# Low-rank network: two inner blocks side by side in TensorE's rows, ranks made twice, row steps two slots apart, and the later statistics taken there

## The reference

```
x = x + ratio_attention(layernorm(x))        # layer 0, causal, score = dot*dot / (|q|^2 + |k|^2 - 2 dot)
x = x + lowrank_ffn(layernorm(x))            # layer 0
x = x + zeroed_attention(layernorm(x))       # layer 1, masked scores are zeroed, not dropped
x = x + ternary_ffn(layernorm(x))            # layer 1, weights rounded to -1, 0, 1
```

```
P = layernorm(x) @ U1          # 256 -> 64
H = gelu(P @ V1 + b1)          # 64 -> 1024
out = (H @ U2) @ V2 + b2       # 1024 -> 64 -> 256
```

## Time and profile before

| | us |
|---|---|
| median of 3 executions | 3095.98 (3095.21 to 3100.54) |
| the profiled execution | 3089.9 |
| its span, first to last instruction | 3088.2 |
| first DMA issue of the low-rank stage | 1312.3 |
| first instruction of the zeroed attention | 1635.3 |
| first dot products of the zeroed attention | 1663.8 |

### The profile page before, as it was taken

How to read it: one execution, slowest core, us unless ns; L and a number is a source line. 1 busy time by engine, 2 the same in 40 slices (tenths; PEclk the granted TensorE clock), 3 DMA queues, 4 the chain that set the end, 5 groups by cost and what they waited for, 6 DMA issues and landing times. The chain is left out here.

```text
span 3088.2 us, 76579 instructions
## 1 busy us (share of the span) xinstructions
PE 2804.2 (91%) x28474; PEld 1973.6 (64%) x28516; DVE 2346.0 (76%) x6131; ACT 2041.1 (66%) x3686; POOL 1749.8 (57%) x3054
## 2 busy tenths in 40 slices
PE   5999999999999999879996888888888889699998
PEld 3777777777777777623333666666666667466666
DVE  6999999999999998753225666676666766399998
ACT  5999999999999999722331555555555555377776
POOL 4767776666666666532111555555555555466664
PEclk8999999999999999989997999999999999799999
DMA  4433443333343333110003544454535453000001
GB/s 108 72 72 73 72 72 72 71 70 69 67 71 69 69 61 65 29 46 1 0 0 72 85 83 75 76 82 79 79 73 86 70 87 65 2 8 28 21 22 35
DMA packets 110034, 181.96 MB, mean 59 GB/s; under 512 B 26720, under 2 KB 96096, under 8 KB 97568
## 3 DMA queue, kind: packets, MB, share of 16 engines
q1 hardware_dynamic: 106208, 176.28, 31.3%
q10 hardware_dynamic: 3456, 0.79, 0.2%
HBM read 115.92 MB, written 60.29 MB: 57 GB/s over the span
## 5 line engine op out<-in xcount | busy, mean ns | idle before, releaser
L792 POOL TENSOR_TENSOR ratio_scores<-ratio_scores,ratio_max_cols 128x512 f32<-128x512 f32 (+3 forms) x1024 | 729.0, 729 | 318.9 <-DVE ratio_max_cols L702 316.7
L1297 DVE TENSOR_REDUCE zeroed_max_cols<-bank 128x1 f32<-128x512 f32 (+3 forms) x1024 | 446.3, 481 | 192.1 <-PE bank L185 190.5
L1189 ACT ACTIVATE zeroed_prob<-bank 128x512 f32<-128x512 f32 x640 | 376.9, 593 | 305.1 <-PE bank L1078 210.1
L182 PE MATMUL bank<-ratio_k_stack,ratio_q_stack 102*128 102x512 bf16 (+7 forms) x2048 | 508.5, 303 | 29.2 <-DVE ratio_max_cols L702 13.3
L702 DVE CUSTOM_DVE_ANT_0 ratio_scores<-bank,ratio_scores 128x512 f32<-128x512 f32 (+3 forms) x1024 | 472.4, 489 | 22.2
L564 ACT ACTIVATE ratio_prob<-bank 128x512 f32<-128x512 f32 x640 | 379.5, 593 | 105.7 <-PE bank L478 105.5
L692 DVE TENSOR_TENSOR ratio_scores<-bank,ratio_inverse 128x512 f32<-128x512 f32 x640 | 435.7, 681 | 17.0 <-PE bank L182 9.8
L1410 POOL TENSOR_SCALAR_AFFINE_SELECT zeroed_prob<-zeroed_prob 128x256 f32<-128x256 f32 (+1 forms) x640 | 228.2, 365 | 338.5 <-ACT zeroed_prob L1189 336.9
L475 PE MATMUL bank<-const_f_sb,ratio_scores 128*128 128x128 f32 x2560 | 410.0, 274 | 0.7 <-ACT ratio_prob L564 0.7
L185 PE MATMUL bank<-const_b_sb 128*128 128x128 bf16 x2048 | 391.7, 223 | 0.0
L553 ACT ACTIVATE ratio_inverse<-bank 128x512 f32<-128x512 f32 x640 | 382.4, 598 | 12.6 <-PE bank L185 12.5
(11 more groups left out here) (169 smaller groups left out, 5574.4 us busy)
## 6 DMA issues: line engine op xcount, KB each, us to landing
ratio_q_stack<-ratio_parts_q SPq DMA_DIRECT2D x186, 128.0 KB
ratio_k_stack<-ratio_parts_k SPq DMA_DIRECT2D x186, 128.0 KB
zeroed_q_stack<-zeroed_parts_q SPq DMA_DIRECT2D x186, 128.0 KB, 4.4
zeroed_k_stack<-zeroed_parts_k SPq DMA_DIRECT2D x186, 128.0 KB, 7.5
ratio_parts_q<-ratio_parts SPq DMA_DIRECT2D x96, 128.0 KB
ratio_parts_k<-ratio_parts SPq DMA_DIRECT2D x96, 128.0 KB
zeroed_parts_q<-zeroed_parts SPq DMA_DIRECT2D x96, 128.0 KB
zeroed_parts_k<-zeroed_parts SPq DMA_DIRECT2D x96, 128.0 KB
```

Of the source, the lines that this page charges most:

```text
L182: i = e.matmul(bank[:, off:off + w], qs[0:rows, s, hh, ib * P:(ib + 1) * P], ks[0:rows, s, hh, 0:w], start=(k == 0), stop=mask is None, sk ...
L792: i = e.tensor_tensor(seg, seg, mx[:, pair % M_BUFS, c:c + 1].to_broadcast([P, w]), ALU.subtract)
L1189: e.activation(prob[:, n % FOLD_PROBS, 0:wd], exp_banks[n % 2][:, 0:wd], ACT.Exp, scale=0.25).then_inc(s["prob"])
L1297: i = e.tensor_reduce(mx[:, pair % FOLDS, c:c + 1], bank[:, off:off + (ib + 1) * P], AX_X, ALU.max)
```

## The change

- `up` now runs in every second slot and issues two matmuls: block f from partitions 0 to 63 of V1 and P, block f+1 from partitions 64 to 127, into two different banks. V1 is loaded twice, into both halves of the partitions. U1 is loaded twice side by side, so that `rank` makes P twice, in partitions 0 to 63 and 64 to 127 (a weight of 128 instead of 64 columns), and `keep_rank` copies 128 partitions. There are four banks for the inner blocks instead of two, and two instead of four for `down`.
- A row's preparation moves from slots 1, 2, 3 to slots 2, 4, 6, `out` from 3, 4 to 3, 5, and there are four buffers for normalised tiles instead of two, so both `normal` of a row run in slots 0 and 1. `keep_sums` stands ahead of the preparation.
- Weight steps are now in the odd slots from the second row on.
- The mean and variance that the zeroed attention needs are taken by DVE at the end of each row in the low-rank stage (slots 4 and 7), and no longer in the zeroed attention. There ACT's root moves from slot 5 to slot 1 and `normal` from slots 6, 9 to 5, 8.

```diff
-Z_STATS_AT, Z_ROOT_AT, Z_XN_AT, Z_TURN_AT, Z_VALUES_AT, Z_SPLIT_AT, Z_SUFFIX_AT, Z_GATHER_AT = (1, 2), 5, (6, 9), (8, 11), (0, 3), (13, 16), 19, 19
+Z_ROOT_AT, Z_XN_AT, Z_TURN_AT, Z_VALUES_AT, Z_SPLIT_AT, Z_SUFFIX_AT = 1, (5, 8), (8, 11), (0, 3), (13, 16), 19
...
                 if half % 2 == 0 and half + 2 < halves:
-                    if at in Z_STATS_AT:
-                        net.pair_stats(q, half // 2 + 1, Z_STATS_AT.index(at), net.stats_in, s["bn_stats"], s["bn_aggr"])
...
-            for pair in range(2):
-                net.pair_stats(q, 0, pair, net.stats_in, s["bn_stats"], s["bn_aggr"])
...
-    PREP_AT = {"xa": 1, "xb": 2, "rank": 3}
+
+    PREP_AT, OUT_AT, STATS_AT = {"xa": 2, "xb": 4, "rank": 6}, (3, 5), (4, 7)
...
-        if b < B - 1:
-            return 4 * b + f - 4 if f >= 4 else -1
-        return 4 * (B - 1) + f if f < FC else -1
+        return 4 * (b - 1) + f // 2 if b and f % 2 else -1
...
-        h_banks, prep_bank, post_bank, down_banks = bk[0:2], bk[2], bk[3], bk[4:8]
-        loaded = 16 * 7
+        h_banks, prep_bank, post_bank, down_banks = bk[0:4], bk[4], bk[5], bk[6:8]
+        loaded = 16 * 9
...
-                    i = e.matmul(prep_bank[0:RANK, :], u1[:, c, :], xnT[:, b % 2, c, :], start=(c == 0), stop=(c == 1))
+                    i = e.matmul(prep_bank[:, :], u1[:, c, :], xnT[:, b % 2, c, :], start=(c == 0), stop=(c == 1))
...
-                q.wait_ge(s["gelu"], n - 1)
-                e.matmul(h_banks[n % 2][:, :], v1[:, f * P:(f + 1) * P], rank_in[:, b % 2, :],
-                         start=True, stop=True).then_inc(s["up"])
+                q.wait_ge(s["gelu"], n - 2)
+                for k in range(2):
+                    rows = slice(k * RANK, (k + 1) * RANK)
+                    i = e.matmul(h_banks[(n + k) % 4][:, :], v1[rows, (f + k) * P:(f + k + 1) * P], rank_in[rows, b % 2, :],
+                                 start=True, stop=True)
+                i.then_inc(s["up"])
...
-                q.wait_ge(s["prep_filled"], prep[b, "xa"] if pair else prep[b - 1, "xb"] if b else 0)
+                q.wait_ge(s["prep_filled"], prep[b - 1, ("xa", "xb")[pair]] if b else 0)
...
             for n in range(n_slots + FC):
                 b, f = divmod(n, FC)
+                if b and f == 2:
+                    keep_sums(b - 1)
                 if b + 1 < B:
                     prepare(b + 1, f)
+                if b and f in OUT_AT:
+                    add(b - 1, OUT_AT.index(f))
+                if b and f in STATS_AT:
+                    pair = STATS_AT.index(f)
+                    q.wait_ge(s["post_read"], post(b - 1, pair))
+                    net.pair_stats(q, b - 1, pair, net.stats_out, s["out_stats"], s["out_aggr"])
                 if n < n_slots:
                     quantise(weight_step(n))
-                if b and f == 2:
-                    keep_sums(b - 1)
-                if b and f in (4, 5):
-                    add(b - 1, f - 4)
...
-            e.dma_start(u1[:, :, :], args["U1"].rearrange("(c p) r -> p c r", p=P)).then_inc(s["weights"], 16)
-            e.dma_start(v1[:, :], args["V1"]).then_inc(s["weights"], 16)
+            for k in range(2):
+                e.dma_start(u1[:, :, k * RANK:(k + 1) * RANK], args["U1"].rearrange("(c p) r -> p c r", p=P)).then_inc(s["weights"], 16)
+            for k in range(2):
+                e.dma_start(v1[k * RANK:(k + 1) * RANK, :], args["V1"]).then_inc(s["weights"], 16)
```

More of the change, by code:

```diff
@@ L1582, in turn_x @@
                 q.wait_ge(s["prep_read"], prep[b, ("xa", "xb")[pair]] - 1)
-                turn_blocks(e, prep_bank, lambda t: xn[:, t % 2, :], pair, net.ident).then_inc(s["prep_filled"])
+                turn_blocks(e, prep_bank, lambda t: xn[:, t, :], pair, net.ident).then_inc(s["prep_filled"])
             def rank(b):
@@ L1637, in out @@
                 i.then_inc(s["post_filled"])
-            for f in range(4):
-                prepare(0, f)
+            turn_x(0, 0)
+            turn_x(0, 1)
+            rank(0)
             for n in range(n_slots + FC):
                 b, f = divmod(n, FC)
-                if n < n_slots:
+                if n < n_slots and n % 2 == 0:
                     up(n)
@@ L1651, in pe @@
                     quantise(weight_step(n))
-                if b and f in (3, 4):
-                    out(b - 1, f - 3)
+                if b and f in OUT_AT:
+                    out(b - 1, OUT_AT.index(f))
         def act(q):
@@ L1660, in act @@
                 q.wait_ge(s["weights"], loaded)
[L1661 removed]
+                q.wait_ge(s["up"], n // 2 + 1)
                 q.wait_ge(s["down"], (n - H_BUFS) // 2 + 1)
[L1663 removed]
+                e.activation(hidden[:, n % H_BUFS, :], h_banks[n % 4][:, :], ACT.Gelu_apprx_tanh,
                              bias=b1[:, f:f + 1]).then_inc(s["gelu"])
@@ L1692, in keep_rank @@
                 q.wait_ge(s["prep_filled"], prep[b, "rank"])
-                q.wait_ge(s["up"], (b - 1) * FC)
-                e.tensor_copy(rank_in[:, b % 2, :], prep_bank[0:RANK, :]).then_inc(s["prep_read"])
+                q.wait_ge(s["up"], (b - 1) * (FC // 2))
+                e.tensor_copy(rank_in[:, b % 2, :], prep_bank[:, :]).then_inc(s["prep_read"])
             def prepare(b, f):
-                if f in (1, 2):
-                    keep_x(b, f - 1)
                 if f < 2:
                     normal(b, f)
-                if f == 3:
+                if f == PREP_AT["xa"]:
+                    keep_x(b, 0)
+                if f == PREP_AT["xb"]:
+                    keep_x(b, 1)
+                if f == PREP_AT["rank"]:
                     keep_rank(b)
@@ L1734, in dve @@
             e.reciprocal(scale[:, :], scale[:, :]).then_inc(s["scale"])
-            for f in range(4):
-                prepare(0, f)
+            normal(0, 0)
+            normal(0, 1)
+            keep_x(0, 0)
+            keep_x(0, 1)
+            keep_rank(0)
             for n in range(n_slots + FC):
                 b, f = divmod(n, FC)
+                if b and f == 2:
+                    keep_sums(b - 1)
                 if b + 1 < B:
                     prepare(b + 1, f)
+                if b and f in OUT_AT:
+                    add(b - 1, OUT_AT.index(f))
[3 more added lines that the diff above has]
+                    net.pair_stats(q, b - 1, pair, net.stats_out, s["out_stats"], s["out_aggr"])
                 if n < n_slots:
                     quantise(weight_step(n))
-                if b and f == 2:
-                    keep_sums(b - 1)
-                if b and f in (4, 5):
-                    add(b - 1, f - 4)
         def pool(q):
```

30 lines of the change are left out of this document (15 added, 15 removed).

## The result

| | before | changed kernel |
|---|---|---|
| median of 4 executions, us | 3095.6 (3092.45 to 3100.54) | 2969.23 (2964.26 to 2970.16) |
| profiled execution, us | 3089.9 | 2970.16 |
| its span, us | 3088.2 | 2968.4 |
| start to the low-rank stage, us | 1312.3 | 1317.3 |
| low-rank stage | 322.9 | 262.3 |

The ratio is 0.9594, 95% interval [0.9574, 0.9614]: 4% faster. The forecast was 2984.5, range 2958 to 3020. A stage counts from its first DMA or table load to that of the next. The first stage has the same code before and after; it took 1312 to 1318 us in the profiles of this case, so its 5.0 us are no effect of the change, and stages shouldn't be read finer than that. The span fell by 60.6 + 63.2 + 1.0 - 5.0 = 119.8 us.

A forecast was written before the change was run, and what follows sets the result against it. PE's queue was taken to bound low-rank rows, DVE the heads of zeroed-attention rows. Gains 62 + 7.5 - 2 + 44 = 111.5 from 3089.9 gave 2978.4; with the median 6.1 above, 2984.5 us, range 2958 to 3020.

The forecast's parts named there:

- Up pairs: Low-rank stage: a pair of ups side by side costs 1.10 us; row 13.65 against 17.52, 62 us gained in 16.
- The covers named: Low-rank row: waits cost nothing; `keep_rank` lies under a down, gelus under down and up, DVE's row 7.3 of 13.65 us.
- Rivals 1 and 2: Low-rank up pairs: 1, staggered by half a matmul, 1.48 us, 3009, chance 0.12; 2, no overlap, 1.91, 3036, chance 0.08.
- Weights and POOL: Early low-rank rows: of 23.5 us, 12 of POOL stalls and 4 from DVE's weight steps remain; net gain 7.5.
- Start and statistics: Low-rank stage: first rank 1.2 us later, first gelu 1, loss 2; last row's statistics move 1.0 us, nothing gained.
- Zeroed attention: Attention rows: 1.98 us of DVE statistics removed, 29.7 in 15 rows, plus 14 from the clock; 44 (25 to 58).
- rival 3: Zeroed attention: another wait refills PE's idle time and the clock still falls; 44 becomes 10, 3018 us, chance 0.10.
- Rival 4: Low-rank stage: PE drops to 1.2 GHz for whole rows, 13.65 us more each; all 16 give 3203, chance 0.03.

The follow-up runs named there:

- series kernel: The changed kernel, but both ups of a pair use partitions 0 to 63 of V1 and P; 3017.23 us.
- four kernels: Statistics in the attention with `normal` late 3025.27 us, early 2991.13; statistics in the low-rank stage with `normal` late 2976.9, early (changed kernel) 2969.23.
- kernel with waits of 1.5 us: The changed kernel with only the attention's slots of root and `normal` put back to 5 and 6, 9; 2976.9 us.

## Why the prediction was right, and where its sizes were off

*Up pairs: right.* 1.06 against 1.10 taken, between ends of 1.05 and 1.91. The row is 13.48 against 13.65: 4.04 less than before, times 16 = 64.6 us (62 forecast). The covers named held: DVE has 7.23 of 13.48 us, and PE waits for `keep_rank` 1.0 us in the whole stage. Rivals 1 and 2 are refuted by the 1.06, and the series kernel, which has the same order of steps and 1.92 a pair, shows that the different rows of the array do it. The first rival read a pair of 1.48 out of the rule in the Trainium skill, "TensorE: Matmul & The Clock Gate", Part 3, that matmuls start and end in program order; the 1.06 does not bear out that reading.

*Weights and POOL: the step that failed.* The forecast came out near the measured time, but this term did not: I forecast that 12 + 4 us of stalls would be left of 23.5; the ranks say 24.8.

Timeline of the changed kernel, ranks of rows 2 and 5, in answer to the earlier trace rows:

```profile
1354.57 1.98 PE L1582 MATMUL bank<-lowrank_xn_T,lowrank_u_twice 128*128 128x512 f32 x4
...
1419.77 1.99 PE L1582 MATMUL bank<-lowrank_xn_T,lowrank_u_twice 128*128 128x512 f32 x4
```

1419.77 - 1354.57 = 65.20, less 3 x 13.48 = 24.8. The windows between these ranks in the changed kernel, and between those of rows 2 and 4 before:

```profile
1354.57:1419.77 65.20, 49.45 (x163) 18.24 (x161) 46.34 (x62) 15.20 (x24) 37.81 (x9) 0.82 0.02 7
```
```profile
1346.69:1405.19 58.50, 43.23 (x110) 15.18 (x108) 35.75 (x25) 10.99 (x16) 33.90 (x8) 0.80 0.02 7
```

PE is idle for 65.20 - 49.45 = 15.8 us; the other 9 are PE's work made slower by the lower clock (0.82 over the stretch). Before, 15.3 of the 23.5 were idle, at 0.80. I had read the 23.5 as waiting alone and had no term for the clock behind it. What stands between the ranks on POOL and DVE:

```profile
1374.24 5.44 POOL L1774 TENSOR_SCALAR ternary_w_negative<-ternary_w_loaded,ternary_w_threshold 128x2048 f32<-128x2048 f32 x1
...
1376.89 8.24 DVE L1680 TENSOR_SCALAR lowrank_xn<-x,mean_var,lowrank_x_scale 128x256 f32<-128x256 f32 x4
...
1379.84 4.50 POOL L1778 TENSOR_TENSOR ternary_w_positive<-ternary_w_positive,ternary_w_negative 128x2048 f32<-128x2048 f32 x1 [0.15 <-POOL ternary_w_negative L1774]
...
1384.54 1.11 PE L119 MATMUL bank<-const_f_sb,lowrank_xn 128*128 128x128 f32 x4 [5.10 <-DVE lowrank_xn L1680]
...
1398.18 12.34 DVE L1680 TENSOR_SCALAR lowrank_xn<-x,mean_var,lowrank_x_scale 128x256 f32<-128x256 f32 x4
...
1411.18 2.07 PE L1634 MATMUL bank<-lowrank_v_twice,lowrank_rank_out 128*128 128x256 f32 x4 [2.55 <-DVE lowrank_rank_out L1726]
```

I had priced the comparisons by their position and left out what follows them. The subtraction starts 0.15 us after them, where POOL added b2 in between before:

```profile
1391.67 5.46 POOL L1765 TENSOR_SCALAR ternary_w_negative<-ternary_w_loaded,ternary_w_threshold 128x2048 f32<-128x2048 f32 x1
1399.91 2.35 POOL L1754 TENSOR_TENSOR x<-x,lowrank_b 128x1024 f32<-128x1024 f32 x1 [2.77 <-DVE lowrank_xn L1680]
1402.22 4.50 POOL L1769 TENSOR_TENSOR ternary_w_positive<-ternary_w_positive,ternary_w_negative 128x2048 f32<-128x2048 f32 x1
```

That left DVE 2.8 us without POOL. And all four `normal` stand in one place now, so the hold goes on for 8.24 and 12.34 us until POOL is done, with `keep_sums` behind it. A row of 13.48 also has less of its own work to lay beside the same 15 us of POOL. The spread kernel, which changes nothing but the positions of the weight steps, lets PE wait for 1.7 us only in all rows from the first comparison on, keeps the clock at 1.00 there, and its stage is 23.3 us shorter. It moves DVE's long steps as well as POOL's, so how much of the 23.3 is POOL's alone is not shown. The Trainium skill, "SBUF — State Buffer", section "Who interferes with whom", says that `tensor_scalar` can contend with POOL in its two-port modes, and that the one that comes second is then blocked wholly, while an instruction with one SBUF input outside such a mode does not contend. The trace agrees: `normal` takes 12.34 instead of 1.35, the adds from PSUM 0.69 in both.

*Start and statistics.* The first rank stands 9.70 us after the stage's start, 8.09 before: 1.6 (1.2 forecast). The statistics, which I put at nothing, cost 4 to 5 us: the stage takes 257.4, 258.1 and 258.3 us in the three kernels without them, 262.3 with them. 1.0 is the tail, which I had as moved. Most of the rest is in the rows of POOL's holds: the ranks of rows 2 and 5 are 62.50 and 62.05 us apart in the first two, 65.20 in the changed kernel. The balance of the stage, with that cost inside the 24.8 (1.3 more than 23.5), is 64.6 - 1.3 - 1.6 - 1.0 = 60.7; measured 60.6. That it closes so well is chance, since two parts that it leaves out cancel. The six rows from rank 4 to 10 before stood 7.7 us above undisturbed ones and the five from rank 5 to 10 now 4.3, a gain of 3.4. As much is lost up to rank 2, where the clock is 0.77 over 37.3 us (8.6 us of full clock missing) and was 0.85 over 34.4 before (5.2).

*Zeroed attention: right in kind, 19 too little.* The row fell from 62.56 to 58.40 us (roots of nine rows, 1723.46 to 2190.68), 4.16 x 15 = 62, of which I had 1.98 + 0.95. The windows of 800 us divide that: 12.79 rows with 55.2 us of PE's work and 7.32 of idle time each before, 13.70 rows with 53.4 and 4.95 now. The clock's part came whole and not by half: 1.8 a row, where 1.9 was my upper end (the two rows against the two above would give 2.3, with shorter rows than the average in the second). And 2.4 instead of 1.98 of idle time went. `normal` also moved ahead of the group of heads; I had named that as a change of long waits into short ones and priced it at nothing. By the four kernels it is worth 8 to 14 us with the statistics gone and 34 with them there, mostly through the clock. No wait as long has come in its place: the largest total after the change, in the same 800 us, is

```profile
PE bank L1086 <- POOL zeroed_m_parts L1396: 18.7, 27, 1.0
```

where PE waited 12.1 us for the same before. That is the mechanism of rival 3, another wait that takes up the idle time, but with 6.6 us of it and not the 34 that the rival needed.

*Rival 4* did not occur: the clock is 1.00 in the undisturbed row with two short streams side by side.

The forecast was 15 us above the median: 19 from the attention, 1 from the ternary stage, less 7 in the low-rank stage and 5 in the unchanged first one, and about 7 because this profiled execution and the median lie otherwise to each other (2970.16 is the highest of four; before, 3089.9 was below the lowest).

Open: which of two things keeps the clock at 0.99 in the kernel with waits of 1.5 us, the shorter wait or the busier time before it. No run told these apart.

## What to carry to other kernels

Where PE binds, two float32 matmuls of 64 contraction rows in different partitions cost as much as one here (1.06 against 1.05 us); look at how many rows of the array each matmul uses before looking for gaps. A wait of PE can cost twice, as idle time and by the clock behind it: try to split or shorten the longest one first, even by order alone. And when PE's row gets denser, price every block of fixed length on another engine again (here POOL's 15 us against DVE's `normal`): in this kernel it cost as much as before. Put it right behind the instructions that it would hold.

## What the runs showed of the hardware that was not expected

- Two float32 matmuls of 64 rows side by side in different rows of the array take 1.06 us, one alone 1.05, two in the same rows 1.92.
- Added PE work made a kernel faster: 1.4 us more a row, 28 us less in all, since the granted clock went from 0.96 to 1.00 (the windows above).
- One wait of 1.8 us a row for `normal` (23.1 us in 800), with 17.6 us more in waits of up to 0.6 us, went with a clock of 0.96; the same DVE work with 27.3 us in waits of up to 0.8 us went with 1.00. Which counts, the longest wait or the smaller sum, is not shown by these two alone.
- DVE's `bn_stats` from SBUF ran in its usual time (two in 0.74 us) beside POOL's comparison, where `normal` was held until POOL was done (timeline of the changed kernel):

```profile
1375.95 0.74 DVE L107 BATCH_NORM_STATS2 stats_out<-x 128x6 f32<-128x256 f32 x2
```
